# Attention values through DRAM, inverse roots on ScalarE, and new engine orders in a six-layer local transformer

## The reference

```python
q, k, v = jnp.split(shift_tokens(x) @ Wqkv, 3, -1)      # 128 -> 3 x 1024
q, k = l2norm(q) * qs, l2norm(k) * ksc                  # over each head's 64 channels
q = q * cos * scale + rotate_half(q) * sin * scale      # k with 1/scale
out = local_attention(q, k, v)                          # each window sees itself and the one before
x = out @ Wo + x
xn = layernorm(shift_tokens(x)) * g + bln
a, gate = jnp.split(xn @ W1 + b1, 2, -1)
x = a * gelu(gate) @ W2 + b2 + x
```

## Time and profile before

| | |
|---|---|
| median of 3 runs | 4286.13 us (4285.91 to 4290.7) |
| the profiled execution | 4280.82 us, span 4279.0 us |
| TensorE busy | 3858.3 us (90% of the span) |
| VectorE busy | 3268.7 us (76%) |
| ScalarE busy | 2674.6 us (63%) |
| GpSimd busy | 2307.6 us (54%) |
| mean granted TensorE clock | 0.937 of full speed |

### The profile page before, as it was taken

The page is one execution under the profiler, slowest core; times in us unless marked ns, Lnnn a source line. Parts: engine busy times, 40 slices in busy tenths (PEclk is TensorE's granted clock), DMA queues, the critical chain, the costliest instruction groups (busy, mean ns, idle before and its releaser), DMA issues.

```text
span 4279.0 us, 147347 instructions
## 1 busy us (share of the span) xinstructions
PE 3858.3 (90%) x60944; PEld 3115.9 (73%) x60944; DVE 3268.7 (76%) x6191; ACT 2674.6 (63%) x4819; POOL 2307.6 (54%) x2140
## 2 busy tenths in 40 slices
PE   4747553899999999999999999999999999999997
PEld 3635542688777778777777777788778777887775
DVE  4385676788888888888888888888888888888883
ACT  2322113577777777777777777777777777777774
POOL 0000001666666666666666666666666666666661
PEclk9666555899999999999999999999999999999998
DMA  1000000222222222223222222222222222222221
GB/s 59 22 28 7 8 12 9 69 72 58 56 56 67 71 57 57 56 57 84 57 58 57 55 67 72 56 57 57 68 73 57 57 58 56 66 74 59 63 60 36
DMA packets 155650, 231.96 MB, mean 54 GB/s; under 512 B 48352, under 2 KB 58336, under 8 KB 153312
## 3 DMA queue, kind: packets, MB, share of 16 engines
q1 hardware_dynamic: 154976, 222.41, 21.3%
HBM read 29.28 MB, written 4.19 MB: 8 GB/s over the span
## 4 chain that ended last, share of the span: by engine, by line
PE 59%; SPq 8%; issue 5%; POOL 4%; ACT 3%; DMA 3%; DVE 2%; ACTq 0%; POOLq 0%; DVEq 0%
PE bank L1519 16%; SPq L965 8%; PE bank L1642 8%; PE bank L1575 6%; PE bank L1556 6%; PE bank L1615 6%; PE bank L1683 4%; PE bank L1630 4%; PE bank L1599 3%; PE bank L1692 3%; DMA vw<-v 3%; POOL qk L1034 2%; PE bank L1569 1%; POOL qk L1044 1%; ACT v L1135 1%
## 5 line engine op out<-in xcount | busy, mean ns | idle before, releaser
L1034 POOL TENSOR_TENSOR qk<-rot_a,rot_b 128x512 f32<-128x512 f32 x768 | 984.5, 1282 | 723.4 <-PE bank L1556 529.6
L1044 POOL TENSOR_TENSOR qk<-qk,rn 128x512 f32<-128x512 f32 x768 | 801.8, 1055 | 141.0 <-DVE rn L73 141.0
L1339 DVE TENSOR_TENSOR rot_a<-bank,rot 128x512 f32<-128x512 f32 x768 | 526.3, 685 | 355.4 <-PE bank L1519 344.1
L1112 ACT ACTIVATE sq<-bank 128x512 f32<-128x512 f32 x768 | 462.9, 603 | 384.5 <-DVE rot_b L1346 363.6
L1354 DVE TENSOR_REDUCE ss<-sq 128x8 f32<-128x512 f32 x768 | 513.6, 669 | 124.6 <-ACT sq L1112 124.4
L1519 PE MATMUL bank<-w_hi,xs_hi 128*128 128x512 f32 x1152 | 560.8, 487 | 25.8 <-POOL xs_lo L1024 17.6
L1053 POOL TENSOR_TENSOR pr<-pr,prec 128x512 f32<-128x512 f32 x384 | 403.7, 1051 | 319.3 <-DVE prec L1374 319.3
L1346 DVE TENSOR_TENSOR rot_b<-bank,rot 128x512 f32<-128x512 f32 x768 | 522.2, 680 | 0.0
L1556 PE MATMUL bank<-ident,qk 128*128 128x128 f32 x3072 | 468.8, 275 | 31.2 <-POOL qk L1044 26.2
L1519 PE MATMUL bank<-w_lo,xs_hi 128*128 128x512 f32 x1152 | 458.9, 398 | 0.0
L1556 PEld LDWEIGHTS bank<-ident,qk 128*128 128x128 f32 x3072 | 370.1, 141 | 121.4 <-POOL qk L1044 45.7
(11 more groups left out here) (245 smaller groups left out, 7584.2 us busy)
## 6 DMA issues: line engine op xcount, KB each, us to landing
vw<-v SPq DMA_DIRECT2D x2880, 64.0 KB, 2.0
stage<-in_wqkv SPq DMA_DIRECT2D x6, 1536.0 KB, 6.6
stage<-in_wb_all SPq DMA_DIRECT2D x6, 1088.0 KB, 5.5
stage<-in_band SPq DMA_DIRECT2D x6, 512.0 KB, 5.3
d_xt<-in_x SPq DMA_DIRECT2D x4, 512.0 KB, 4.2
base_scratch<-d_res SPq DMA_DIRECT2D x4, 512.0 KB, 2.7
out<-stage SPq DMA_DIRECT2D x16, 128.0 KB, 2.1
stage<-base_scratch SPq DMA_DIRECT2D x1, 1664.0 KB, 7.1
```

What stands on the lines that cost most here:

```text
L1034: nc.gpsimd.tensor_tensor(qk[:, c, :], rot_a[:, c % 2, :], rot_b[:, c % 2, :], ALU.add)\
L1044: nc.gpsimd.tensor_tensor(y, y, rn[:, x.q, 8 * c:8 * c + 8].unsqueeze(2).to_broadcast([P, 8, DH]), ALU.mult).then_inc(S["scaled"], 1)
L1112: nc.scalar.activation(sq[:, :], proj_bank(x, c)[:, :], ACT.Square).then_inc(S["squared"], 1)
L1339: nc.vector.tensor_tensor(rot_a[:, c % 2, :].rearrange("p (h d) -> p h d", h=8), proj_bank(x, c)[:, :].rearrange("p (h d) -> p h d", h=8), ...
```

## The change

**Values.** `window` first writes half of `v` (128 x 1024, 512 KB) to a scratch tensor in DRAM, waits for that on SyncE, and reads it back into `vw` by four transfers of 192 or 256 KB instead of 14 or 16 of 64 KB. `value_out` waits only for the write of the half that it overwrites.

**Roots.** `inverse_roots` is replaced by `floors` (DVE), `roots` (ACT: Ln, then Exp of -0.5 times it, on 128x66) and `polish` (DVE: one Newton iteration, three instructions). Behind the three Gelus a load of the table set `natural_log_exp_and_others` is written out.

**Orders.** The lists of PE, ACT, DVE and POOL are rearranged. The end of the old body on PE (`turn_qk` 7, `turn_probs` 2, `score` 1, `shift` 0, `turn_heads` 1) moves to the start of the next body, where the same item has its next name. The matmul `shift` is kept.

```diff
+POLISH = 3
+EXP_LN_TABLE = "natural_log_exp_and_others"
...
         def landed(x, half):
-            k = 2 * x.u + half
-            return 16 * sum(HALF_DMAS[i % 2] for i in range(k % SLOTS, k + 1, SLOTS))
+            return 64 * ((2 * x.u + half) // SLOTS + 1)
...
+                kept = v_d[x.u % 2, :, :]
+                sp.dma_start(kept[half * P:(half + 1) * P, :], v[:, half, :]).then_inc(S["v_kept"], 16)
+                sp.wait_ge(S["v_kept"], 16 * (2 * x.u + half + 1))
                 for r in range(2):
                     for a in range(2):
                         rows = slice(r * KEYS + a * WIN, r * KEYS + (a + 1) * WIN)
-                        cols = slice(r * CK, (r + 1) * CK)
-                        for w in range(4):
-                            n, c = (half, w) if a == 1 else (half, w - 1) if w else (half - 1, 3)
-                            if n >= 0:
-                                sp.dma_start(vw[rows, slot(x, half), w, r, :], v[c * WIN:(c + 1) * WIN, n, cols])\
-                                    .then_inc(S[f"vw_in{slot(x, half)}"], 16)
+                        w = 0 if a == 1 or half == 1 else 1
+                        first, last = half * P + (w + a - 1) * WIN, (half + 1) * P + (a - 1) * WIN
+                        sp.dma_start(vw[rows, slot(x, half), w:4, r, :],
+                                     kept[first:last, r * CK:(r + 1) * CK].rearrange("(w p) n -> p w n", p=WIN))\
+                            .then_inc(S[f"vw_in{slot(x, half)}"], 16)
...
POOL, body:
-                if turn.there:
-                    low_half(new, "added", turn.u * 8 + 7)
+                if out.there:
+                    low_half(new, "normed", out.u * 4 + 3)
...
+                add(turn, 6)
+                scale(turn, 0)
                 add(turn, 7)
-                scale(turn, 0)
                 scale(turn, 1)
+                add(new, 0)
                 scale(turn, 2)
-                add(new, 0)
+                scale(turn, 3)
+                scale(turn, 4)
+                norm(out, 3)
                 add(new, 1)
-                norm(out, 3)
-                scale(turn, 3)
                 add(new, 2)
                 norm(att, 0)
-                scale(turn, 4)
                 add(new, 3)
                 scale(turn, 5)
-                add(new, 4)
                 norm(att, 1)
                 scale(turn, 6)
+                add(new, 4)
                 add(new, 5)
+                scale(turn, 7)
                 norm(att, 2)
-                scale(turn, 7)
-                add(new, 6)
...
ACT:
-                if n == 0 and before.there:
-                    need(act, S[f"vw_in{slot(before, 0)}"], landed(before, 0))
-                    need(act, S[f"vw_in{slot(before, 1)}"], landed(before, 1))
+                if n % 2 == 0 and before.there:
+                    need(act, S["v_kept"], 16 * (2 * before.u + n // 2 + 1))
...
+            def roots(new, out):
...
+                nc.scalar.activation(ss_log[:, :], ss[:, :], ACT.Ln).then_inc(S["logged"], 1)
+                need(act, S["logged"], new.u + 1)
+                need(act, S["scaled"], min(new.u - 1, NSEQ * DEPTH) * 8)
+                need(act, S["rstd_spread"], out.u - 1)
+                nc.scalar.activation(rn[:, new.q, :], ss_log[:, :], ACT.Exp, scale=-0.5).then_inc(S["rooted"], 1)
...
gelu, behind the three Gelus:
+                nc.scalar.preload_act_table_set(EXP_LN_TABLE)
...
ACT, body, behind high_half(b, new):
+                square(turn, 7)
...
+                value_out(att, out, 3)
...
+                turned_out(att, 6)
+                roots(turn, ffn)
                 exp(out, 3)
+                heads_out(out, 0)
                 probs_out(out, 2)
+                turned_out(att, 7)
                 heads_taken(out, 1)
-                heads_out(out, 1)
-                turned_out(att, 7)
-                exp(att, 0)
                 square(new, 0)
...
+                exp(att, 0)
                 turned_out(turn, 0)
                 affine(ffn)
+                heads_out(out, 1)
                 heads_taken(out, 2)
                 turned_out(turn, 1)
                 square(new, 1)
...
+                value_out(turn, att, 0)
                 gelu(ffn)
-                value_out(turn, att, 0)
-                turned_out(turn, 2)
                 square(new, 2)
...
                 probs_out(out, 3)
-                turned_out(turn, 3)
+                turned_out(turn, 2)
                 exp(att, 1)
                 value_out(turn, att, 1)
+                turned_out(turn, 3)
                 square(new, 3)
...
DVE:
+            def polish(new, out):
...
+                need(dve, S["rooted"], new.u + 1)
+                nc.vector.tensor_tensor(rn_t[:, :], y, y, ALU.mult).then_inc(S["rn_steps"], 1)
+                need(dve, S["rn_steps"], n + 1)
+                nc.vector.scalar_tensor_tensor(rn_t[:, :], rn_t[:, :], -0.5, ss[:, :], ALU.mult, ALU.mult).then_inc(S["rn_steps"], 1)
+                need(dve, S["rn_steps"], n + 2)
+                nc.vector.scalar_tensor_tensor(y, rn_t[:, :], 1.5, y, ALU.add, ALU.mult).then_inc(S["rn_steps"], 1)
...
-                top(att, 1)
+                total(out, 3)
                 deviate(ffn)
                 sum_squares(new, 0)
                 rotate(new, 1, 0)
+                total(att, 0)
                 rotate(new, 1, 1)
-                total(out, 3)
+                sum_squares(new, 1)
+                top(att, 1)
...
-                top(turn, 0)
+                top(att, 3)
                 sum_squares(new, 7)
...
-                inverse_roots(new, out)
+                floors(new, out)
+                top(turn, 0)
+                polish(new, out)
...
PE, body:
                 query_key(b, new, 0)
-                weigh(out, 2)
+                turn_qk(att, 7)
+                turn_probs(out, 2, att, 3)
+                score(att, 1)
+                shift(att, 0)
                 spread(ffn)
                 turn_qk(turn, 0)
+                turn_heads(out, 1)
+                query_key(b, new, 1)
+                weigh(out, 2)
+                turn_qk(turn, 1)
+                ffn_in(ffn, 1)
                 value(b, turn, 0)
-                query_key(b, new, 1)
-                turn_qk(turn, 1)
                 ffn_in(ffn, 0)
-                ffn_in(ffn, 1)
+                query_key(b, new, 2)
                 turn_qk(turn, 2)
-                query_key(b, new, 2)
                 score(att, 2)
                 shift(att, 1)
+                turn_probs(out, 3, turn, 0)
                 ffn_in(ffn, 2)
-                turn_probs(out, 3, turn, 0)
-                turn_qk(turn, 3)
-                shift(att, 2)
                 query_key(b, new, 3)
-                ffn_out(ffn)
                 value(b, turn, 1)
                 weigh(out, 3)
+                turn_qk(turn, 3)
                 turn_heads(out, 2)
+                ffn_out(ffn)
                 turn_probs(att, 0, turn, 1)
                 query_key(b, new, 4)
                 turn_qk(turn, 4)
+                turn_heads(out, 3)
+                shift(att, 2)
                 weigh(att, 0)
-                turn_heads(out, 3)
                 value(b, turn, 2)
-                turn_qk(turn, 5)
                 query_key(b, new, 5)
                 join_heads(b, out)
-                turn_output(b, ffn, turn.u * 8 + 6)
+                turn_output(b, ffn, turn.u * 8 + 5)
+                turn_qk(turn, 5)
                 query_key(b, new, 6)
                 score(att, 3)
-                turn_probs(att, 1, turn, 2)
...
                 mean(out)
+                turn_probs(att, 1, turn, 2)
                 turn_heads(att, 0)
                 query_key(b, new, 7)
-                score(turn, 0)
                 value(b, turn, 3)
-                turn_qk(turn, 6)
                 variance(out)
                 weigh(att, 1)
+                turn_qk(turn, 6)
+                score(turn, 0)
                 shift(att, 3)
-                turn_qk(turn, 7)
-                turn_probs(att, 2, turn, 3)
-                shift(turn, 0)
-                score(turn, 1)
-                turn_heads(att, 1)
```

More of the change, by code:

```diff
@@ L29 @@
 SLOTS = 3
-HALF_DMAS = (14, 16)
 NNORM = 64
@@ L1057, in body @@
                 new, turn, att, out, ffn = b.items
[L1058 to L1059 removed]
+                if out.there:
+                    low_half(new, "normed", out.u * 4 + 3)
+                elif att.there:
+                    low_half(new, "scaled", att.u * 8 + 8)
+                elif turn.there:
+                    low_half(new, "added", turn.u * 8 + 6)
                 else:
                     low_half(new, "prepared", NPREP)
+                add(turn, 6)
+                scale(turn, 0)
                 add(turn, 7)
[L1063 removed]
                 scale(turn, 1)
+                add(new, 0)
                 scale(turn, 2)
[L1066 removed]
+                scale(turn, 3)
+                scale(turn, 4)
+                norm(out, 3)
```

(58 more changed lines are left out.)

16 lines of the change are left out of this document (9 added, 7 removed).

## The result

The changed kernel takes 4229.68 us (median of 4 runs, 4226.37 to 4231.09), the kernel before 4286.83 us in the same comparison. The ratio is 0.9864 with a 95% interval of 0.9847 to 0.9881: 1.4% faster, by far more than the 0.2% that can be told apart. The prediction was 4230 us.

A forecast was written before the change was run, and what follows sets the result against it. TensorE was taken to bound the 86-body loop. Terms of -79.6, +25.8, -3, -4 and +5 make -55.8 from 4280.8, so 4225.0, and 5.3 for the median gives 4230 us; likeliest 4215 to 4247 us (0.50).

The forecast's parts named there:

- The bound: Pipeline loop of 86 bodies: TensorE bounds it, floor 35.28 us a body, so any reordering gives at most about 80 us.
- new wait: Each body: TensorE's query_key(new, 3) waits for square(new, 2), 0.3 us (0 to 0.6), +25.8 us in all.
- Values: Value copy on ScalarE: its DMA wait goes; a half reaches vw 7 to 18 us after its copy, hidden by slack.
- Roots: Chain ahead of spread: the scaled-chunk wait goes; turn_qk(turn, 0) and spread find their input with 1.5 to 2 us to spare.
- The table load: ScalarE behind the Gelus: load, Gelus, load and square take 4.4 us against TensorE's 4.0, opening a 0.2 to 0.4 us wait.
- layer switches: Conversions of the five layer switches in the pipeline: each keeps about 1 us, +5 us in the sum.
- fill, up to the 6th spread: Five bodies of the pipeline's fill: 0.6 us less each, -3 us in the sum.
- drain, from the 92nd spread: Pipeline's drain: one value wait of 2.70 us and one root wait of 3.07 us, -4 us in the sum.
- through the rest of the body I find 0.5 us or more of room ahead of each TensorE step: Body outside the table-load stretch: at least 0.5 us of room ahead of each TensorE step.
- The rule of the Trainium skill: Table switch behind the Gelus: a drain of about 1.38 us each; as the slower rival, 4349 us, chance 0.10.
- The rival with no new wait at all: query_key(new, 3) finds its square in time, so waits close altogether: 4204 us, down to 4191, chance 0.15.
- That the change does nothing: Whole kernel: new waits eat the 0.92 us a body that is won; 4284 us, within 0.2%, chance 0.06.

The follow-up runs named there:

- run 5: Changed kernel with its written-out table load moved from behind the Gelus to ahead of the Exp of unit 1: 4186.25 us, ratio 0.9766.
- run 8: Changed kernel with both the table load and the last layer's output transposes moved later: 4176.04 us, ratio 0.9740.
- run 10: Kernel before, old orders, with values through DRAM and the new roots placed behind the attention's Exp of unit 3: 4207.62 us, ratio 0.9832.
- Run 1: Kernel before with values through DRAM alone, old orders and old roots: 4247.31 us, ratio 0.9918.
- Run 2: Kernel before with the roots on ScalarE alone, ahead of the attention's Exp of unit 3, old orders and values: 4277.46 us, ratio 0.9992.
- Run 7: Changed kernel with the last layer's output transposes behind score 3, their add and its wait later too: 4217.25 us, ratio 0.9838.
- run 3: Changed kernel with old value transfers and old eleven-step roots, so new orders alone, second table load placed by the compiler: 4411.69 us, ratio 1.0312.
- run 6: Changed kernel with the eleven-step roots back on VectorE, table load kept behind the Gelus: 4323.61 us, ratio 1.0088.
- run 11: run 8 with the eleven-step roots back, without Ln, Exp and the written-out load: 4270.69 us, ratio 0.9978.
- run 4: Changed kernel with the old value transfers back, new roots and orders kept: 4656.01 us, ratio 1.0863.

## Why the prediction was right, step by step

**The bound.** That TensorE bounds the loop, that only its waits can be won, and that a body without them takes 35.28 us, was right for the full bodies: runs 5, 8 and 10 have bodies of 35.27 to 35.30 us. That it is the most that any reordering can give was not: run 5 gained 95 us between the profiled executions, 31 of them in the fill and the drain. The reading that an idle time costs more than the trace gives for it was right too. It was not carried through, though, to the new wait (below).

**Values.** Write 2.6 us, reads 3.7 and 4.9, hidden: right, and the 8.8 to 13.9 us to `vw` lie in the 7 to 18 that the prediction gave. Run 1 gives the part's worth.

**Roots.** The walk from `query_key(new, 0)` agrees with the trace to about 0.1 us at each step, and the wait went. Run 2 shows that this depended on the place of the two activations on ScalarE, which the prediction did not weigh.

**The table load.** The place, the instruction that waits and the mechanism were right. The gap was 0.2 us, as computed, but it acts on the body as 0.41 us; the term had 0.3.

**The sum**, term by term against the two profiled executions (spans 4279.0 and 4229.3 us):

| term | predicted | measured | from |
|---|---|---|---|
| waits of 86 bodies | -79.6 | -79.6 | floor confirmed by run 5 |
| new wait | +25.8 | +34.4 | 86 x (35.68 - 35.28) |
| layer switches | +5 | +4.8 | 6th to 80th spread: 2645.1 us less 74 x 35.68 |
| output in the last layer | none | +12.5 | 80th to 92nd spread: 440.7 us less 12 x 35.68 |
| fill, up to the 6th spread | -3 | -13.6 | 1026.7 to 1013.1 us |
| drain, from the 92nd spread | -4 | -8.3 | 138.7 to 130.4 us |
| together | -55.8 | -49.8 | spans differ by 49.7 |

The step that failed is "through the rest of the body I find 0.5 us or more of room ahead of each TensorE step": the walk was made for a body of the first five layers, and `turn_output`, which the diff moves ahead of `turn_qk(turn, 5)` with the wait for its add, was left out. Run 7 shows its worth, 12.4 us. The new wait was also sized too small, by 8.6 us. Against both stands what the sum missed on the other side. Before the first spread 11.9 us are won, where the sum had nothing. The matmuls of `spread`, before and then after (count, shortest, median and longest in ns, first and last start):

```profile
L1667 PE MATMUL bank<-ident,rn x384: 275/275/582, 846.5 to 4262.2; 128*128 128x128 f32 x192
```

```profile
L1697 PE MATMUL bank<-ident,rn x384: 272/275/579, 834.6 to 4212.5; 128*128 128x128 f32 x192
```

The first projection of the transformer, which follows the unchanged parts, starts at 717 to 722 us from run to run. Counted from it, the first spread comes after 128.2 us before and 113.5 after, after 120.8 us in run 3 (orders alone), 118.9 in run 6 (orders and values), 130.2 in run 1 and 125.5 in run 2. So about half of these 15 us is the new orders' and most of the rest the short roots'; which of the moved steps does it was not tried. The prediction looked only at bodies in which all five stages are present.

**The rivals.** The rule of the Trainium skill (ScalarE: Activation LUTs, What ACT_TABLE_LOAD costs), a drain of about 1.38 us at every switch, did not come true here: the load behind the Gelus starts 0.02 us after their end, and the square 0.01 us after the load. The rival with no new wait at all, 4204 us, is what one gets by moving the load: run 5 gives 4186 us, lower since fill and drain bring 31 us where the sum had 7, although the last layer keeps the 12 us of the wait that was left out. That the change does nothing was out.

**What the parts are worth.** The new orders as such, with both other parts present, made it slower: 4229.7 us against 4207.6 in run 10. With the load and the output placed well they bring 26 us against run 10 by the profiled executions (spans 4178.0 and 4204.0) and 32 us by the medians. Of the 26, 9.8 lie before the first spread, 8.2 in the drain, the rest mostly at the layer switches, and next to nothing in the ordinary body (35.27 against 35.30 us).

## What to carry to other kernels

In a pipeline bound by one engine, measure a body without waits first: its length is the floor, and the difference times the number of bodies is all that any reordering can bring in the full bodies. Count a new wait on the bound engine at the difference that it makes between bodies, here the idle time that the trace names and 0.2 to 0.4 us on top for each wait. A table load, or any other step on a side engine, belongs where nothing that the bound engine needs stands behind it. Moving it by three places brought 43 us here, more than either part by itself in the old orders. And walk the special bodies (fill, last layer, drain) too: here they held 34 us, 22 won and 12 lost.

## What the runs showed of the hardware

A wait of 0.16 us named ahead of a projection made each body 0.41 us longer (35.68 against 35.27 us). The same holds in the kernel before, where 0.23 us of idle time go with 0.50 us, in run 11 (0.41 us idle, 0.77 us longer) and in run 6 (0.58 us idle in two waits, 1.19 us longer). The excess is 0.25 to 0.36 us for each wait in these four, so it is the short waits that the idle time understates most. Where it comes from was not shown.

An explicit table load costs its 1.28 us and no more, and Ln and Exp then share the set: still two loads a body with three functions in use.

In run 4 TensorE's granted clock had a mean of 0.93 to 0.96 over stretches of 400 us in which it was busy 374 to 377 us, while in run 3, busy 377 to 386 us of 400, it rounds to 1.00. Each of the 71 falls among the 86 bodies of run 4 began 0.3 to 2.4 us after the start of a TensorE wait of 1.1 to 1.5 us, 59 times the one for a Gelu. The four matmuls of `ffn_in` behind it took 2.04 us (the row in run 4), and 1.10 us behind the same wait in the body from 1562.86 us, which held the full clock. But a wait of more than 1 us does not always bring a fall: all 86 bodies of run 4 have one, and 40 bodies of run 3, of which 3 have a fall. What decides between them stays open.
